# The keys and values of the context, computed inside the first scan of a decoder layer in place of ahead of it

## What is computed

```
x = layernorm(x + mamba_and_mlp(x))
x = layernorm(x + cross_attention(x, ctx))
x = layernorm(x + lora_ffn(x))

mamba:  xz = rmsnorm(x) @ in_proj.T ; causal conv, silu ; dt, B, C from x_proj
        h[t] = exp(dt*A) * h[t-1] + dt*B*u ;  y = sum_n h*C + u*D ;  y * silu(z) @ out_proj.T
cross_attention:  K = ctx @ Wk.T + bk ;  V = ctx @ Wv.T + bv      (4 x 64 x 512 each)
        Q = x @ Wq.T + bq ; scores of 16 heads ; a learned temperature per head from their
        mean, maximum and entropy ; softmax ; @ V ; @ Wo.T + bo
```

## Time and profile before

| | |
|---|---|
| time, median of 3 runs | 4376.36 us (4375.86 to 4382.17) |
| the profiled execution | 4379.0 us, of which the span of the profile is 4377.2 us |
| busy share of the span | PE 85%, DVE 58%, POOL 57%, ACT 49% |
| mean granted TensorE clock | 0.901 of 2.4 GHz |
| DMA | 483.17 MB, 110 GB/s over the span |

### The profile page before, as it was taken

How to read it: one execution, slowest core, us unless ns; L and a number is a source line. 1 busy time by engine, 2 the same in 40 slices (tenths; PEclk the granted TensorE clock), 3 DMA queues, 4 the chain that set the end, 5 groups by cost and what they waited for, 6 DMA issues and landing times.

```text
span 4377.2 us, 36093 instructions
## 1 busy us (share of the span) xinstructions
PE 3725.6 (85%) x9848; PEld 1749.1 (40%) x9848; DVE 2522.7 (58%) x3319; ACT 2161.6 (49%) x5177; POOL 2488.3 (57%) x1100
## 2 busy tenths in 40 slices
PE   6555999799979988899999998899998988899677
PEld 3111434343334334544344334534444333544344
DVE  2665478657756883367735885267744886122211
ACT  3443454565465454556526555466526554443344
POOL 0998399649954993079914994059932996000000
PEclk9555999899989998899999998899999998899788
DMA  4333344334523541144423442134423442112000
GB/s 147 115 113 101 104 155 156 111 120 154 164 95 113 164 157 59 63 140 144 152 86 111 155 153 77 63 121 147 146 84 103 160 154 89 40 57 67 25 21 28
DMA packets 221267, 483.17 MB, mean 110 GB/s; under 512 B 31884, under 2 KB 32268, under 8 KB 220812
## 3 DMA queue, kind: packets, MB, share of 16 engines
q1 hardware_dynamic: 221068, 480.87, 34.3%
HBM read 470.82 MB, written 9.96 MB: 110 GB/s over the span
## 4 chain that ended last, share of the span: by engine, by line
PE 54%; POOL 16%; DVE 12%; issue 8%; ACT 8%; DMA 1%; SPq 0%; POOLq 0%; DVEq 0%; ACTq 0%
PE ps L1490 28%; POOL hb L961 10%; DVE hb L1296 6%; POOL hb L951 6%; PE ps L1579 5%; PE ps L1548 5%; PE ps L1591 5%; PE ps L1658 1%; PE ps L1624 1%; PE ps L1603 1%; PE ps L1541 1%; PE ps L1518 1%; ACT ps L1171 1%; PE ps L1670 1%; PE ps L1559 1%
## 5 line engine op out<-in xcount | busy, mean ns | idle before, releaser
L951 POOL TENSOR_TENSOR hb<-dtu,bc 128x1024 f32<-128x1024 f32 x512 | 1205.6, 2356 | 73.3 <-PE ps L1591 31.0
L961 POOL TENSOR_TENSOR hb<-hb,bc 128x1024 f32<-128x1024 f32 x512 | 1205.6, 2355 | 60.7 <-ACT state L1086 35.4
L1490 PE MATMUL ps<-fT,wden 128*128 128x512 f32 x2304 | 1053.6, 607 | 28.6 <-DVE hm L1334 21.1
L1010 ACT ACTIVATE ps<-dt,a_neg 128x512 f32<-128x512 f32 x1024 | 690.9, 688 | 693.3 <-DVE hb L1296 690.2
L1591 PE MATMUL ps<-hb,ident 128*128 128x512 f32 x1024 | 632.4, 706 | 306.3 <-POOL hb L961 303.4
L1490 PEld LDWEIGHTS ps<-fT,wden 128*128 128x128 f32 x2304 | 444.2, 195 | 597.2 <-issue 596.4
L1296 DVE TENSOR_TENSOR_SCAN hb<-ps,state,hb 128x512 f32<-128x512 f32 x512 | 626.7, 1266 | 14.1 <-ACT ps L1010 7.2
L1296 DVE TENSOR_TENSOR_SCAN hb<-ps,hb 128x512 f32<-128x512 f32 x512 | 596.2, 1206 | 21.1 <-POOL hb L951 13.4
L1305 DVE TENSOR_TENSOR ps<-ps,hb 128x512 f32<-128x512 f32 x512 | 355.5, 694 | 364.8 <-POOL hb L961 363.9
L1579 PE MATMUL ps<-wden,hm 128*128 128x512 f32 x1024 | 487.7, 623 | 17.5 <-DVE res L1350 12.8
L1490 PE MATMUL ps<-xnT,wmix 128*128 128x512 f32 x1024 | 468.6, 609 | 12.8 <-ACT xnT L1034 8.7
(11 more groups left out here) (192 smaller groups left out, 3894.4 us busy)
## 6 DMA issues: line engine op xcount, KB each, us to landing
bc<-bc_dram SPq DMA_DIRECT2D x1024, 256.0 KB, 3.7
wden<-in_w SPq DMA_DIRECT2D x192, 512.0 KB, 3.7
wmix<-in_w_mix SPq DMA_DIRECT2D x96, 512.0 KB, 3.6
watt<-in_w_qof SPq DMA_DIRECT2D x32, 512.0 KB, 4.3
xm<-in_x SPq DMA_DIRECT2D x8, 1024.0 KB, 5.5
res<-in_x SPq DMA_DIRECT2D x8, 1024.0 KB, 5.6
wden<-in_w_qof SPq DMA_DIRECT2D x16, 512.0 KB, 3.8
out<-res SPq DMA_DIRECT2D x8, 1024.0 KB, 4.3
```

What stands on the lines that cost most here:

```text
L951: TTn(hb[:, k % 4], dtu[:, :, :], bc[:, 0, k % 3].unsqueeze(1).broadcast_to([P, 2, CH]), ALU.mult).then_inc(s.s1_ready, 1)
L961: TTn(hb[:, k % 4], hb[:, k % 4], bc[:, 1, k % 3].unsqueeze(1).broadcast_to([P, 2, CH]), ALU.mult).then_inc(s.s3_done, 1)
L1010: A_(dst, dt[:, p % 2, jj], ACT.Exp, scale=a_neg[:, j, n:n + 1]).then_inc(full_of(key), 1)
L1490: ins = M(dst, a, b, start=start and n == 0, stop=stop and n == len(pairs) - 1)
```

## The change

The prologue's keys and values become units of the y stream, ahead of chunk 0's MLP: `("key", 0, c4)` and `("value", 0, b)`. The planner places them on PE, ACT and DVE; they use the four common PSUM banks. SP issues x first, then the constants, the first three blocks of mixer weights, and only then the context, Wk, Wv and bv, which now go into buffers that nothing else uses so early (xw, two slots of res, hm). The stores, the wait for them and `load_kv(0)` become a unit of SP's list (`kv_store`), placed by the planner's time for the last value; `load_kv(1)` is placed one planned microsecond later. The results are staged in qT. The core of the diff:

```diff
 def y_plan():
-    got = []
+    got = [("key", 0, c4) for c4 in range(KC)] + [("value", 0, b) for b in range(BATCH)]
...
+    if kind == "key":
+        part(PE, 2 * MM, ("proj", 0), takes=(u,))
+        part(ACT_, 0.5, mine(), gives=(u,))
+    elif kind == "value":
+        part(PE, 4 * MM, ("proj", 0), takes=(u,))
+        part(DVE, EV, mine(), gives=(u,))
...
-    for b in range(1, BATCH):
-        got.append((DONE[("woa", 2 * b - 3, TT - 1)] + 1 if b > 1 else 1.0, 2, ("kv_load", b)))
+    kept = DONE[("value", 0, BATCH - 1)]
+    got += [(kept, 2, ("kv_store", 0)), (kept + 4, 2, ("kv_load", 0)), (kept + 5, 2, ("kv_load", 1))]
+    for b in range(2, BATCH):
+        got.append((DONE[("woa", 2 * b - 3, TT - 1)] + 1, 2, ("kv_load", b)))
...
+            def store_kv():
+                for c4 in range(KC):
+                    emptied(sp, ("key", 0, c4))
+                for b in range(BATCH):
+                    emptied(sp, ("value", 0, b))
+                for c4 in range(KC):
+                    sp.dma_start(k_dram[:, c4].rearrange("b p k -> p b k"), kT[:, c4].rearrange("p (b k) -> p b k", b=BATCH)
+                                 ).then_inc(s.kv_stored, 16)
+                for b in range(BATCH):
+                    sp.dma_start(v_dram[b], vR[:, b]).then_inc(s.kv_stored, 16)
+                sp.wait_ge(s.kv_stored, 16 * 2 * BATCH)
+
             load_x(0)
+            for dst, src in ((ident[:, :], A["identity"]), (e64[:, :], A["e64"]), (w_ra[:, :, :], A["w_ra"]),
...
+                sp.dma_start(dst, src).then_inc(s.const_in, 16)
             for m in range(3):
                 load_mix(0, m)
+            sp.dma_start(ctxT, A["ctxT"].rearrange("p (c k) -> p c k", c=KC)).then_inc(s.ctx_in, 16)
+            sp.dma_start(res[:, 1], A["wk"]).then_inc(s.ctx_in, 16)
+            sp.dma_start(res[:, 2], A["wv"]).then_inc(s.ctx_in, 16)
+            sp.dma_start(hm[:, 1], A["bv"].partition_broadcast(P)).then_inc(s.ctx_in, 16)
             for n in range(YSLOTS):
                 load_y(n)
-            sp.wait_ge(s.kv_stored, 16 * 2 * BATCH)
-            load_kv(0)
...
+                elif kind == "key":
+                    A_(kT[:, i], filled(act, unit)[:, 0:BATCH * KEYS], ACT.Identity, bias=bk_c[:, i:i + 1]).then_inc(free_of(unit), 1)
...
+                elif kind == "value":
+                    V.tensor_tensor(vR[:, i], filled(dve, unit)[0:KEYS], hm[0:KEYS, 1], ALU.add).then_inc(free_of(unit), 1)
...
-            dve.wait_ge(s.kv_stored, 16 * 2 * BATCH)
```

More of the change, by code:

```diff
@@ L269, in parts @@
     elif kind == "sc1":
-        part(PE, TURN, ("query", c, last), ("kv", b), takes=(u,))
+        part(PE, TURN, ("query", c, last), ("kv", b), ("value", 0, BATCH - 1), takes=(u,))
     elif kind == "mx":
@@ L687, in decoder_layer @@
         zt = spt[:, 1]
+        ctxT = xw[:, 0:1024].rearrange("p (c k) -> p c k", c=KC)
+        kT = qT[:, 0].rearrange("p (c k) -> p c k", c=KC)
+        vR = qT[0:KEYS, 1:3].rearrange("p a (b d) -> p (a b) d", d=DM)
         def sp_e(j):
@@ L777, in _ @@
         def _(sp):
[L778 to L789, removed]
             def load_mix(c, m):
@@ L868, in load_kv @@
                                  ).then_inc(kv_in[r], 16)
[L871 to L879, removed]
@@ new lines, in _ @@
+            load_x(0)
+            for dst, src in ((ident[:, :], A["identity"]), (e64[:, :], A["e64"]), (w_ra[:, :, :], A["w_ra"]),
+                             (w_b[:, :], A["w_b"]), (w_dt[:, :], A["w_dt"]), (cols[:, :], A["cols"]),
+                             (a_neg[:, :, :], A["a_log"]), (t_w1[:, :], A["t_w1"]), (t_w2[:, 0:HID], A["t_w2"]),
+                             (t_w3c[:, :], A["t_w3"]), (t_b[0:HID, 0:1], A["t_b1"]), (t_b[0:HID, 1:2], A["t_b2"]),
+                             (t_b[:, 2:3], A["t_b3"].partition_broadcast(P)), (f_sc[:, :], A["f_sc"])):
+                sp.dma_start(dst, src).then_inc(s.const_in, 16)
@@ L920, in _ @@
                     load_wf(c)
+                elif kind == "kv_store":
+                    store_kv()
                 elif kind == "kv_load":
@@ L994, in _ @@
             A_(ln1[:, :], zero3[:, 0:1], ACT.Ln, bias=ones_t[:, 0:1]).then_inc(s.act_consts, 1)
[L995 to L998, removed]
             act.wait_ge(s.act_consts, 2)
@@ L1115, in _ @@
                         A_(fT[:, c4], filled(act, key), ACT.Copy, scale=norm2[:, c4:c4 + 1]).then_inc(free_of(key), 1)
+                elif kind == "key":
+                    A_(kT[:, i], filled(act, unit)[:, 0:BATCH * KEYS], ACT.Identity, bias=bk_c[:, i:i + 1]).then_inc(free_of(unit), 1)
                 elif kind == "hg":
                     src = filled(act, ("h1", c, i))
+                    if c == 0 and i == 1:
+                        emptied(act, ("value", 0, BATCH - 1))
                     if i >= FG:
@@ L1152, in _ @@
                 elif kind == "query":
+                    if c == 0 and i == 0:
+                        act.wait_ge(s.kv_stored, 16 * 2 * BATCH)
                     if c > 1 and i == 0:
@@ L1240, in _ @@
             V.tensor_scalar(conv_w, conv_w, 0.5, None, ALU.mult).then_inc(s.dve_consts, 1)
[L1241 to L1245, removed]
             dve.wait_ge(s.act_consts, 2)
@@ L1491, in group @@
                 return ins
-            pe.wait_ge(s.ctx_in, 64)
             pe.wait_ge(s.const_in, 16 * CONSTS)
             pe.wait_ge(s.zeroed, 8)
[L1496 to L1504, removed]
             pe.wait_ge(s.dve_consts, 2)
-            w = None
             for unit in ORDER[PE]:
@@ L1560, in _ @@
                         ins.then_inc(full_of(key), 1)
+                elif kind in ("key", "value"):
+                    pe.wait_ge(s.ctx_in, 64)
+                    dst = take(pe, unit)
+                    wi = res[:, 1 + (kind == "value")]
+                    if kind == "key":
+                        ins = group(dst[:, 0:BATCH * KEYS], [(wi[:, ci, i * P:(i + 1) * P], ctxT[:, ci]) for ci in range(KC)])
+                    else:
+                        ins = group(dst[0:KEYS], [(ctxT[:, ci, i * KEYS:(i + 1) * KEYS], wi[:, ci]) for ci in range(KC)])
+                    ins.then_inc(full_of(unit), 1)
                 elif kind in ("h", "hv"):
```

4 lines of the change are left out of this document (2 added, 2 removed).

## The result

The changed kernel takes 4339.68 us (median, 4336.82 to 4341.45) against 4376.11 us of the kernel before (4374.93 to 4382.17), run beside it: a ratio of 0.9913, with a 95% interval of 0.9896 to 0.9931, so 36.4 us less. Its profiled execution has a span of 4335.0 us. The prediction was 4345.1 us, 31.3 less than before, with a range of 4338 to 4357.

A forecast was written before the change was run, and what follows sets the result against it. POOL was taken to pace chunk 0's scan and PE to be busy most of the time behind it; 36.4 us gained less a 5.1 us stall gave 31.3, thus a median of 4345.1 us, range 4338 to 4357.

The forecast's parts named there:

- The front starts earlier: Prologue: with x loaded first, ACT's squares of x start at 12.9 in place of 49.29, 36.4 us gained.
- The cost of the products: Between `dt` and chunk 0's first sum: 22.57 us of PE products are hidden, costing 0, at most 0.7 us.
- half clock at the prologue's start: Key and value products' 22.57 us in the prologue were said to contain half-clock time, covering a 0.8 us bank wait.
- The stall in the scan: Chunk 0's scan: SP's stores, wait and loads issue b(6) 9.3 us late, so POOL stalls 5.1 us.
- The hidden hold: Rival: POOL, late anyway in chunk 0's scan, hides the stall to net 0 to 3 us; chance 0.09.
- The long hold: Rival: slow small-row loads ahead of B's rows stall chunk 0's scan 10 to 18 us; chance 0.10.
- Waiting late: SP's queue in chunk 0's scan: waiting later for the stores' landing would take 1.8 us off the stall.
- The sum up to chunk 0: To the end of chunk 0's scan: 36.4 us gained less 5.1 us of stall, 31.3 us.
- A shift passes on one to one: Behind chunk 0's scan: all later work moves by the same shift; wrong if that stretch changes over 4 us.
- Slower by the clock: Rival: shifted PE idle stretches bring 80 us more at low clock behind chunk 0, over 0.2% slower; chance 0.02.

The follow-up runs named there:

- the uncovered kernel: Changed kernel with key and value units moved ahead of the first turn on PE and behind the norm on ACT and DVE; 4364.58 us.
- the hold taken away: Changed kernel with SP's store of keys and values, the wait for it and both loads moved behind chunk 0's scan; 4338.97 us.

## Why the prediction came out as it did

The measured 4339.68 us lies in the stated range, and the gain of 36.4 us is 5 more than the 31.3 of the forecast. The mechanism held up to the end of chunk 0's scan: there the forecast's terms can be compared one by one.

- *The front starts earlier, 36.4.* 35.9 at the squares and 35.6 at `du`; the turn took 5.63 us and 5.28 before, which is the other 0.3. The step was right, and its parts are 25.1 for the products and 10.5 for the rest of the change, with the order of loads of the kernel whose products stand uncovered.
- *The cost of the products, 0, at most 0.7.* 0: with a quarter of them the scan's end moves by less than 0.1 us. Their 21.7 us are more than the 18.8 us of idle PE and z gate that stood between `dt` and the first sum, so the first sum began 2.9 us later, counted from `du`; sum 0 was still done 2.4 us before POOL took up b(4). Without that cover `du` is 25.1 us later. The "half clock at the prologue's start" that the prediction names is not in the rows of the granted clock: they read 1.00 from 0 to 44 us in the trace before. What the rows do show is that the keys' products took 8.68 us as PE's first work and 7.17 in their new place.
- *The stall in the scan, 5.1.* Somewhat too small: 6.3 in the first trace, 5.9 in the second. b(6) was issued 0.7 us later than forecast, and 4.94 us (4.43 in the second trace) went by from there to POOL's start where the sum had 4.47. That 4.47 was misread from chunk 4. POOL's product at 2173.75 waited for the row that SP issued at 2167.89, and not for the next one at 2169.28. SP's queue there, and the answer on the row of 2167.89, with who waited for it (us, times) and its landing:

```profile
2167.01 0.84 SPq L825 DMA_DIRECT2D wden<-in_w  x2
2167.89 0.87 SPq L843 DMA_DIRECT2D bc<-bc_dram  x1
```

```profile
  POOL hb L951: 2.2, 1
DMA to landing us min/median/max: 5.8/5.8/5.8
```

So chunk 4's figure is 5.86 us, and there two loads of MLP weights stood ahead of the row besides the six small ones. With 5.86 the sum would have given a stall of 6.4. That 4.47 came so near to the 4.43 to 4.94 of the changed kernel is luck, and chunk 4 was less like this case than the prediction took it to be.
- *The hidden hold.* Part of this rival is in the runs: with the hold taken away, POOL has a sixth wait for ACT of 1.2 us, so that only 5.2 of the 6.3 come back. Measured against the kernel before, which has five waits for ACT of 6.7 us in all, as the changed kernel has, the scan is 6.5 us longer (318.7 against 312.2).
- *The long hold.* It rested on loads of keys and values landing in 4.9 us. In chunk 0's scan of the changed kernel they landed in 2.2 (kbd) and 2.7 us (vbd), by the medians. The Trainium skill (DMA: Bandwidth & Descriptors, Specifications) gives 512 bytes as the least size for the full rate. The changed kernel's trace agrees as far as it goes: 64 KB in rows of 128 bytes landed in 2.7 us, as long as a store of 128 KB in rows of 2 KB took (2.6). A fixed time per transfer would look the same, and no run tells the two apart. It did not reach the path as the rival had it: POOL's wait before b(6) was 5.6 to 6.2 us in every trace with the same order of issues.
- *Waiting late.* The 1.8 us of waiting, which the prediction puts down to the trace, were its own sum; the changed kernel's trace has 2.0 us from the end of the last store's issue to the first load (94.67 to 96.67). No run takes away this wait alone.
- *The sum up to chunk 0, 31.3.* 29.1 between the first traces; 30.3 if the three ends of scan 0 before and the two after are averaged (421.9 against 391.65).
- *A shift passes on one to one.* This is the step that was too simple. The prediction treated 4379.0 and 2.6 us as all there is of an execution's own, and wrote that it is wrong if the stretch behind chunk 0 changes by more than 4 us. It changed by 13.1. But that sign could not tell: it changes by 16.9 in one and the same program. Of the measured 36.4, the 5 us above the forecast are inside that scatter, so that the total lies so near is in part luck. With all ten runs of the changed kernel (median 4341.1) and all fifty of before (4374.7) the difference is 33.5 us. Four traces with the keys and values in the prologue have a mean rest of 3950.8 us, and ten with them in the planner's lists one of 3946.1. Whether these 3 to 5 us are chance or a small gain behind chunk 0, these runs can't tell.
- *Slower by the clock.* The mechanism of this rival exists, with both signs, but 17 us from end to end where it needed 40.

## What to carry to other kernels

Work that the first stage does not need was free here because the place it moved to had room on two counts: PE had to wait there anyway for most of their 22 us, and the result that it delayed, the first sum, was not wanted by the pacing engine until 2.4 us after it was done. What cost was the part that goes through a queue in order: eight issues, a wait for their landing and six more issues, in the queue that feeds the pacing engine, cost that engine 6 us, and the same block a stage later cost none of such waits. Before a price is taken from another place of the trace, make sure which transfer the engine there waited for: the one issued last before it went on need not be it. Where the total scatters by more than the step is worth, take the verdict from the stretch in the trace that the edit moves, and a second trace of the same kernel before explaining what moved elsewhere.

## What the hardware did that I had not expected

One program's time behind chunk 0 varied between 3939.5 and 3956.4 us from one execution to another; PE's busy time varied by 25 us with it (3469.9 to 3494.9), at more or less time at the lower clock, while DVE, ACT and POOL repeated to 1.1 us. An issue on SP isn't a constant either: the load of a row of B was issued in 0.32 to 0.43 us in most places, and behind six small loads in 1.68, 1.32 and 0.62 us in three traces in which the same issues stood ahead of it; two issues of vbd took 4.20 us right behind 4 MB of loads issued from 43.44 on (by the sizes of the issues), and 1.20 to 1.25 in chunk 0's scan. And PE's first work was slow without the granted clock saying so: the turn took 5.63 us as PE's first work and 3.84 right behind the products of the uncovered kernel, and the granted clock reads 1.00 in both stretches.
